# Attention: the value products of two key steps side by side in TensorE's order

## What is computed

```python
scores = jnp.einsum('bhqd,bhkd->bhqk', q, k) / math.sqrt(dh)
scores = scores + alibi_bias(H, L, scores.dtype)[None]      # layer 2: causal mask only
attn = jax.nn.softmax(scores, axis=-1)
out = jnp.einsum('bhqk,bhkd->bhqd', attn, v)
```

## Time and profile before

| what | before |
|---|---|
| median of 3 runs | 2706.49 us (2703.36 to 2708.31) |
| span of the profiled execution | 2709.2 us |
| TensorE busy | 2224.6 us (82%) |
| DVE busy | 1611.4 us (59%) |
| ACT busy | 1261.1 us (47%) |
| POOL busy | 752.8 us (28%) |

### The profile page before, as it was taken

One profiled execution on the slowest core, in us unless ns is written; L12 is line 12 of the kernel. 1 busy time (PEld: TensorE's weight loads), 2 busy tenths in 40 slices (PEclk: granted clock), 3 DMA queues, 4 the chain that ended last, 5 costly groups with the idle time before them and its releaser, 6 DMA issues. The chain is left out here.

```text
span 2709.2 us, 44319 instructions
## 1 busy us (share of the span) xinstructions
PE 2224.6 (82%) x15435; PEld 1297.3 (48%) x15454; DVE 1611.4 (59%) x3356; ACT 1261.1 (47%) x1914; POOL 752.8 (28%) x886
## 2 busy tenths in 40 slices
PE   3787787884698998999989689999997987685674
PEld 1455555563244444444444334444444785444374
DVE  6666676752674675756747787777772443654102
ACT  2334444322255666666565245665665442331143
POOL 1335253543010110200200133424231115662432
PEclk8888988887798999999998699999998998895597
DMA  2112200003021020111100011222213992110285
GB/s 65 41 48 56 49 10 2 3 1 106 32 73 30 20 62 20 38 44 38 56 26 20 19 46 57 80 58 74 63 42 121 318 322 72 39 41 14 80 265 178
DMA packets 144400, 185.07 MB, mean 68 GB/s; under 512 B 27153, under 2 KB 118450, under 8 KB 139159
## 3 DMA queue, kind: packets, MB, share of 16 engines
q1 hardware_dynamic: 103391, 136.81, 17.0%
q0 software_dynamic: 13696, 32.02, 3.8%
q10 hardware_dynamic: 27126, 13.75, 1.8%
HBM read 129.75 MB, written 52.21 MB: 67 GB/s over the span
## 5 line engine op out<-in xcount | busy, mean ns | idle before, releaser
L1766 DVE TENSOR_REDUCE a_mpart<-a_mx 128x1 f32<-128x512 f32 (+3 forms) x1216 | 745.7, 657 | 298.0 <-PE a_mx L1500 167.5
L1674 ACT ACTIVATE a_prob<-a_st 128x1024 f32<-128x1024 f32 (+3 forms) x768 | 608.1, 812 | 517.0 <-PE a_st L1533 370.7
L1497 PE MATMUL a_mx<-a_ka,a_qa 96*128 96x512 bf16 (+3 forms) x1536 | 436.1, 342 | 63.7 <-DVE a_mpart L1766 30.0
L1530 PE MATMUL a_st<-a_qa,a_ka 96*128 96x512 bf16 (+3 forms) x1536 | 420.7, 336 | 26.2 <-ACT a_prob L1674 14.5
L1548 PE MATMUL a_acc<-a_prob,a_v_aug 128*9 128x512 f32 (+3 forms) x3072 | 326.1, 501 | 0.0
L1497 PEld LDWEIGHTS a_mx<-a_ka,a_qa 96*128 96x128 bf16 x1536 | 143.0, 100 | 345.3 <-DVE a_mpart L1766 164.5
L1533 PE MATMUL a_st<-w_mask_t,identb 128*128 128x128 bf16 x1024 | 211.8, 226 | 0.0
L1530 PEld LDWEIGHTS a_st<-a_qa,a_ka 96*128 96x128 bf16 x1536 | 147.5, 100 | 127.0 <-ACT a_prob L1674 26.2
L1421 POOL DMA_INDIRECT x_rows<-l_xn,l_slots x128 | 124.9, 976 | 259.1 <-ACT a_prob L1674 248.6
L2190 PE MATMUL t_psu<-t_xsT,t_w 128*128 128x128 f32 x960 | 155.3, 296 | 23.3 <-DMA t_w<-in_l_experts 17.0
L1500 PE MATMUL a_mx<-w_mask_q,identb 128*128 128x128 bf16 x768 | 167.9, 228 | 0.0
(11 more groups left out here) (457 smaller groups left out, 3987.3 us busy)
## 6 DMA issues: line engine op xcount, KB each, us to landing
t_w<-in_l_experts SPq DMA_DIRECT2D x160, 192.0 KB, 4.4
t_w<-in_l_experts SPq DMA_DIRECT2D x40, 514.0 KB
a_qa<-q_parts_dram SPq DMA_DIRECT2D x96, 192.0 KB
a_ka<-k_parts_dram SPq DMA_DIRECT2D x96, 192.0 KB
x_rows<-zeros SPq DMA_DIRECT2D x25, 512.0 KB, 3.6
t_xs<-x_rows ACTq DMA_DIRECT2D x40, 256.0 KB, 5.2
y_rows<-t_y POOLq DMA_DIRECT2D x40, 256.0 KB
q_parts_dram<-a_parts SPq DMA_DIRECT2D x24, 256.0 KB
```

The source lines that it names most:

```text
L1497: ins = pe.matmul(to, qa[G % NQ][0:QK_PAD, h0 + k, qi * P:(qi + 1) * P], ka[G % NQ][:, h0 + k, lo:hi], start=not masked_first, stop=k == p ...
L1530: ins = pe.matmul(to[:, lo:HALF], ka[G % NQ][:, h, j * P:(j + 1) * P], qa[G % NQ][0:QK_PAD, h, ch * HALF + lo:(ch + 1) * HALF], start=True ...
L1674: act.activation(prob[:, k_at % NP_, 2 * pair:2 * pair + 2, lo:HALF], sring[s % 2][:, :, lo:HALF], ACT.Exp, scale=1.0 if alibi(G // NG) el ...
L1766: dve.tensor_reduce(mpart[:, G % 2, h0:h0 + per, qi, piece], slot[:, 0:per * width].rearrange("p (k w) -> p k w", k=per), X, ALU.max).then ...
```

## The change

The values of an odd and an even step stand next to each other. They come behind the second score of steps 2, 4, 6, 8 and 10; behind steps 1, 3, 5, 7, 9 and 11 stand no values, and the last two keep their place at the group's end.

```diff
-                if s:
-                    order.append(("values", G, *key_steps[s - 1]))
+                if s and s % 2 == 0:
+                    order += [("values", G, *key_steps[s - 2]), ("values", G, *key_steps[s - 1])]
                 if s == 6:
                     order.append(("turn_out", G, 0))
-            order.append(("values", G, *key_steps[-1]))
+            order += [("values", G, *key_steps[-2]), ("values", G, *key_steps[-1])]
```

## The result

| what | before | after |
|---|---|---|
| median | 2704.93 us (2699.27 to 2708.31, 4 runs) | 2757.01 us (2747.04 to 2764.99, 4 runs) |
| ratio to before | | 1.0197, 95% interval 1.0163 to 1.0232 |
| span of the profiled execution | 2709.2 us | 2761.6 us |

The change makes the kernel 52 us slower. The forecast was 2721.4 us with a range of 2694 to 2751. The direction was right; the size was 3.5 times the 14.9 us of the sum, and the time lies 6 us above the range.

What follows compares the result with a forecast made beforehand. TensorE's own work was taken to set a group's length, with DVE close behind through a three-slot ring. The terms -35.2 + 30 + 10.8 + 7.8 + 1.5 = +14.9 us gave 2706.49 + 14.9 = 2721.4 us, range 2694 to 2751.

Steps and rivals of the forecast that it cites:

- the sum: Whole kernel: -35.2 + 30 + 10.8 + 7.8 + 1.5 = +14.9 us, the last +1.5 for the last group.
- The visits: TensorE switching into and out of value products: 0.22 us each, 160 fewer in 32 groups, -35.2 us.
- rival 3: Value pairs keep an inner price of 0.11 us for each visit, +17.6 more, 2739 us; chance 0.15.
- Values 0: Group start: moved from between scores 1b and 2a, their free fill is paid, 1.07 us in group 27, +30 in all.
- Rival 1: TensorE's own time decides and added waits do not come: 2671 us, or 2686 with half of values 0 exposed; chance 0.18.
- Values 2: Moved from between scores 3b and 4a: 0.54 of their 0.64 us becomes waiting; taken for 20 groups, +10.8 us.
- Wide steps: Paired 512-column values leave ScalarE idle, later scores wait for exponentials: 0.39 us in group 27, times 20, +7.8 us.
- Group 27, +0.9: One group without projections: -1.10 + 1.07 + 0.54 + 0.39 = +0.9 us on 31.8.
- Groups with projections there have more TensorE work and need less filling; I take 20 of 32.: Scales the values 2 wait of 0.54 us from a group like 27 to all groups: +10.8 us, bounds 0 and 17.
- Rival 4: Longer waits at group starts lower TensorE's clock: every third group, ten times 1.6 us, +16, 2737 us; chance 0.10.
- the four terms: Whole kernel: saved visits -35.2, values 0 +30, values 2 +10.8 and wide steps +7.8 us.

Runs made afterwards that it cites:

- experiment 1: Against the kernel before: only values 0 move, to values 1 behind score 2b, all other values stay single; 2731.51 us against 2700.78, ratio 1.0128.
- experiment 2: Against the kernel before: only values 4 with 5, 6 with 7 and 8 with 9 paired, values 0 to 3 as before; 2715.57 us, ratio 1.0068.
- the second: Changed kernel and kernel before each run again unaltered, for another profile; 2755.75 and 2714.87 us.
- experiment 5: Against the kernel before: the change's pairs only in the eight groups with layer 1's network, old order elsewhere; 2731.02 us, ratio 1.0084.
- experiments 8 and 9: Layer 1's network's Gelu replaced by a Relu, in the changed kernel and in the old order; 2705.98 us and 2677.92 us.

## Why the prediction was right at full clock and wrong in the network's groups

- **The visits, -35.2 us.** Right where the clock is full. The pairs cost 1.84 and 1.63 us, nothing inside, so rival 3 (0.11 inside) is out.
- **Values 0, +30 us.** Right. turn_max stays at 6.27 us, and experiment 1 gives +0.86 for this pair against the +0.85 worked out, and 0.87 in the mean of the 15 groups at full clock. Rival 1 (TensorE's time decides) falls with it.
- **Values 2, +0.54 in a group like 27.** Nearly right. The change's +0.88, less the first pair's +0.86 and the wide pairs' -0.42, leaves +0.44 for the pair of 2 and 3. With its visit of -0.22 added back that is 0.66 of waiting, if the parts add up.
- **Wide steps, +0.39 in a group like 27.** A little too high: 0.24 in experiment 2, again if the visits are worth 0.22. The 3.7 us that ScalarE was said to need for four wide exponentials are 3.9 by the earlier trace rows.
- **Group 27, +0.9.** Measured +0.88. Over the 15 groups at full clock it is +0.77 each in the mean, and -0.19 in group 21, the sixteenth at full clock.
- **"Groups with projections there have more TensorE work and need less filling; I take 20 of 32."** This step failed, and with it the sum, which had no term for the clock. It set the groups with the network at about -1.10 + 1.07, nothing. They are +5.0 us each in the first profile and +4.5 in the second (436.5 - 400.9 = 35.6 in eight). TensorE has more work in them, but it also waits already, for ScalarE's activations, and the pairs add 2.2 us of waiting in group 11, twice what they add in group 27 (1.5 in the mean of the eight).
- **Rival 4, the longer waits cost clock, comes closest to what happened, at another place and at a greater price.** I had put it at each group's start, at 1.6 us in ten groups, +16. Group 27 keeps 1.00 with 1.3 us of idle time, and the 15 groups keep it too. The clock fell in the groups with the network, where it had already been below 1.00, and there 69 us more at the lower level cost about 35 us. The rows on which I had priced it are of a group without the network, and in the window that holds them (group 25) the clock rose from 0.96 to 1.00 with the change. The views of the network's groups (clock 0.88 to 0.97, waits for a_hT) showed this before the change; the forecast did not go by group there.

The cause of the 52 us is then, in the first profiles: waits added at full clock, less the visits, +11.5; the network's groups +40.3, of which about 35 is lower clock; +5.1 in the others; 4.6 given back elsewhere. Two things are shown by experiments. Pairs in the eight groups alone cost 23 us (experiment 5). And with ScalarE's switches of function taken out (experiments 8 and 9), the extra loss goes from 40 or 36 to 15 us in these groups, while the added waits stay. That the waits are what brings the lower clock is read from this comparison; no run shows the step between the two, and group 6 became 7.4 us longer with no more idle time than before.

**What stays open.** Why the lower clock lasts 3.4 us in one case and 10.2 in another with nearly the same work around it, I can't say. Experiment 5 shows that it is not fixed by the order within the group: it moves from group to group when work earlier in the program changes. So the split between single groups is not predicted by anything that I measured, nor why groups 16 and 17, at 0.80 and 0.77 before, paid nothing. Nor was it tried whether the small products and the Gelu taken out together would leave the plain sum of the four terms.

## What to carry to other kernels

Saving switches on a busy engine by putting like work together takes away the fill that stood between a slow partner's results. Where the wait then comes at the same time as before, the fill is paid in full (1.07 us against 0.22 saved). Read the granted clock by stage before forecasting: in the 15 groups at 1.00 the mean came within 0.15 us of the sum for a group like 27, though single groups lay up to 0.8 from it, and group 21 lay 1.1 from it. In the eight groups with the network, at 0.88 to 0.97, the same edit cost six times as much in the mean, from -0.9 to +8.2 us in single groups. If a stage already waits and its clock is below 1.00, give the clock a term and a wide range there, or leave that stage as it is.

## What the hardware showed that I had not expected

- TensorE at the lower clock can be recorded as busy throughout: 10.20 of 10.20 us at a mean clock of 0.52, with 32 small products (5.65 us instead of 3.76) at its beginning.
- Taking the table loads of the Gelu off ScalarE, 1.28 us each, went with a mean clock of 0.93 in group 11 under the pairs, in place of 0.84, without shortening what the pairs added in waits (2.28 against 2.19 us).
- The same instructions in the same order in one group took 60.56 us in one kernel and 53.18 in another (clock 0.83 and 0.97), while only the order in groups without the network differed between the two.
